# One core, 128 tiles of attention and a feed-forward layer with experts: q, k and up projections made for two tiles at a time

## What is computed

```
x = x + layernorm(attention(layernorm(x)))
x = x + layernorm(ffn(layernorm(x)))

attention(h):  q, k, v = h @ w_q.T, h @ w_k.T, h @ w_v.T
  sq, sk = elu(q) + 1, elu(k) + 1
  memory part: (sq @ memory) / (sq @ memory_norm)
  local part, chunk by chunk of 128 rows: A = (sq @ sk.T) * causal mask
     (A @ v + sq @ S) / (sum(A) + sq @ z);  then S += sk.T @ v, z += sum(sk)
  output (gate mix of the two) @ w_o.T
ffn(h):  silu(h @ W_up.T) @ W_down.T                       (256 -> 1024 -> 256)
       + product-key experts: 4 heads, top 8 of 1024 each,
         weights silu((h . down_embed) * softmax(scores)), sum of up_embed rows
```

## Time and profile before

| | |
|---|---|
| median of 3 runs | 2856.78 us (2856.33 to 2860.16) |
| profiled run: its time, its span | 2860.13 us, 2858.4 us |
| PE, PEld busy | 99%, 80% of the span |
| ACT, DVE, POOL busy | 88%, 85%, 72% of the span |
| granted TensorE clock | 0.998 of full |
| DMA, bytes moved | 471.58 MB, mean 165 GB/s |

### The profile page before, as it was taken

One profiled execution on the slowest core, in us unless ns is written; L12 is line 12 of the kernel. 1 busy time (PEld: TensorE's weight loads), 2 busy tenths in 40 slices (PEclk: granted clock), 3 DMA queues, 4 the chain that ended last, 5 costly groups with the idle time before them and its releaser, 6 DMA issues.

```text
span 2858.4 us, 48065 instructions
## 1 busy us (share of the span) xinstructions
PE 2829.4 (99%) x14724; PEld 2294.9 (80%) x14724; DVE 2424.2 (85%) x6125; ACT 2525.0 (88%) x3618; POOL 2055.1 (72%) x2460
## 2 busy tenths in 40 slices
PE   8899999999999999999999999999999999999999
PEld 6688788878888888888788878888888788788877
DVE  5888888888888888888888888888888888888886
ACT  5888998899888989888998898888989888998997
POOL 3677777777777777777777777777777777777674
PEclk9999999999999999999999999999999999999999
DMA  4576667766766766676667766666767676667664
GB/s 120 140 174 166 166 172 172 167 169 169 170 165 170 171 168 167 169 173 167 165 172 173 167 168 170 168 166 170 171 168 167 169 173 166 167 171 171 151 152 120
DMA packets 450053, 471.58 MB, mean 165 GB/s; under 512 B 234883, under 2 KB 384516, under 8 KB 449796
## 3 DMA queue, kind: packets, MB, share of 16 engines
q0 software_dynamic: 52832, 199.77, 36.1%
q1 hardware_dynamic: 396964, 268.74, 31.1%
HBM read 137.37 MB, written 131.20 MB: 94 GB/s over the span
## 4 chain that ended last, share of the span: by engine, by line
PE 95%; ACT 1%; DVE 1%; issue 1%; POOL 1%; DMA 1%; SPq 0%; POOLq 0%; DVEq 0%; ACTq 0%
PE banks L684 89%; PE banks L828 4%; PE banks L810 2%; POOL sums L532 0%; DMA g_parts<-w_way 0%; DVE w_blocks L1117 0%; DVE prob L1109 0%; DMA wexp<-wexp 0%; ACT prob L979 0%; PE banks L619 0%; PE banks L627 0%; PE banks L641 0%; DMA w_way<-w_blocks 0%; PE banks L661 0%; PE banks L698 0%
## 5 line engine op out<-in xcount | busy, mean ns | idle before, releaser
L532 POOL TENSOR_TENSOR sums<-scores 128x1024 f32<-128x1024 f32 x512 | 1002.3, 2037 | 76.0 <-ACT scores L1018 76.0
L518 POOL TENSOR_TENSOR rstd<-var_eps,minus_half 128x1 f32<-128x1 f32 x512 | 501.9, 980 | 43.0 <-ACT y_sq L928 15.3
L684 PEld LDWEIGHTS banks<-xn2T,wupT 128*128 128x128 f32 x4096 | 484.0, 188 | 9.4 <-DVE state L1171 3.0
L684 PE MATMUL banks<-xn2T,wupT 128*128 128x128 f32 x4096 | 486.2, 274 | 2.1 <-DVE state L1171 2.1
L684 PE MATMUL banks<-deT,xn2T 128*128 128x512 f32 x1024 | 484.4, 596 | 2.4 <-DVE picked L1064 2.0
L684 PE MATMUL banks<-ue,gT 128*128 128x256 f32 x2048 | 462.8, 379 | 0.3 <-ACT gT L957 0.3
L684 PE MATMUL banks<-wdownT,hT 128*128 128x256 f32 x2048 | 462.8, 379 | 0.2 <-ACT y_sb L1014 0.2
L684 PEld LDWEIGHTS banks<-wdownT,hT 128*128 128x128 f32 x2048 | 389.0, 190 | 56.8 <-issue 3.0
L684 PEld LDWEIGHTS banks<-ue,gT 128*128 128x128 f32 x2048 | 388.7, 190 | 52.7 <-ACT gT L957 0.7
L570 POOL TENSOR_TENSOR wexp<-wexp,w_last 128x1 f32<-128x1 f32 x127 | 131.6, 1036 | 385.1 <-ACT z_last L1007 385.1
L684 PEld LDWEIGHTS banks<-deT,xn2T 128*128 128x128 f32 x1024 | 191.9, 197 | 130.9 <-issue 121.2
(11 more groups left out here) (162 smaller groups left out, 6661.2 us busy)
## 6 DMA issues: line engine op xcount, KB each, us to landing
wexp<-wexp POOLq DMA_DIRECT2D x127, 1024.0 KB, 9.1
wexp<-wexp POOLq DMA_DIRECT2D x127, 512.0 KB, 4.7
w_way<-w_blocks SPq DMA_DIRECT2D x127, 512.0 KB, 2.6
g_parts<-w_way SPq DMA_DIRECT2D x508, 128.0 KB, 4.9
xn_way<-xn_blocks SPq DMA_DIRECT2D x248, 128.0 KB, 1.8
x_in<-_attn_hidden_states_dram SPq DMA_DIRECT2D x128, 128.0 KB, 2.2
out_dram<-x_out SPq DMA_DIRECT2D x128, 128.0 KB, 1.8
xn1T<-xn_way SPq DMA_DIRECT2D x500, 32.0 KB, 2.2
```

Source lines behind the costliest of these rows:

```text
L518: return nc.gpsimd.tensor_tensor(rstd[:, n, m:m + 1], var_eps[:, n, m:m + 1], minus_half[:, :], ALU.pow)
L532: return nc.gpsimd.tensor_tensor(sums[:, k, :, :], scores[:, k, 0:XIN].unsqueeze(2).broadcast_to([P, XIN, NKEYS]), scores[:, HEADS + k, :] ...
L684: last = nc.tensor.matmul(out, lhs(c), rhs(c), start=(start and c == 0), stop=(stop and c == chunks - 1))
```

## The change

Three things are done. `PAIRED = 6`: from tile 6 on, tiles (t, t+1) with t even share their q, k and up products, so that an instruction moves 256 columns, the two tiles lying side by side in `xn1T` and `xn2T` (now 4 buffers each, `TURNED`). An even turn of stage 7 makes k for tiles t and t+1; an odd one makes q for t+1 and t+2. The even and the odd turn of stage 10 each make one half of the up product for both tiles of the pair, up to tile 125. Second, `ahead(t, stage)` gives the chain of the first norm the tile of stage-1 instead of stage: from tile 5 on, `xn1` is normed, turned and gathered one turn earlier. Third, on SyncE the gather of `xn2T` stands before `sk_way` and `g_parts`.

```diff
+        def q_buffer(t):
+            return 1 if t < PAIRED else 1 + ((t - PAIRED) // 2 + 1) % 2
+        def ahead(t, stage):
+            old, new = t[stage], t[stage - 1]
+            if old is not None and old < AHEAD:
+                return old
+            return new if new is not None and new > AHEAD else None
+        def paired_up(t):
+            return PAIRED <= t < LATE
...
# SyncE
+            def xn1_in(x):
+                moved(sp, s_xn1_blocks_out, x, 1, TILES, EARLY)
+                wait(sp, s_v_in_psum, x + 1 - TURNED)
+                gather(xn1T[:, x % TURNED, :, :]..., xn1_way[x % 2, :, :], s_xn1_blocks_in[x % 2])
...
# TensorE
+            def up(t, half):
+                if not paired_up(t):
+                    for k in range(4):
+                        ic = 4 * half + k
+                        last = product(u_ps[half][:, k * P:(k + 1) * P], DC, lambda c: wupT[:, c, ic * P:(ic + 1) * P],
+                                       lambda c: xn2T[:, t % TURNED, :, c])
+                else:
+                    first = t // 2 * 2 % TURNED
+                    for k in range(2):
+                        ic = 4 * (t % 2) + 2 * half + k
+                        last = product(two_tiles(u_ps[half])[:, k, :, :], DC, lambda c: wupT[:, c, ic * P:(ic + 1) * P],
+                                       lambda c: xn2T[:, first:first + 2, :, c])
+                return last
+            def two_tile_q_or_k(dst, w, t):
+                for ec in range(DC):
+                    last = product(two_tiles(dst)[:, ec, :, :], DC, lambda c: w[:, c, ec * P:(ec + 1) * P],
+                                   lambda c: xn1T[:, t % TURNED:t % TURNED + 2, :, c])
+                return last
...
+                    if paired_up(u) and u % 2 == 0:
+                        moved(pe, s_xn2_blocks_in, u + 1, BLOCKS, LATE, EARLY)
...
-                    early(pe, 'xn1', t[7])
-                    moved(pe, s_xn1_blocks_in, t[7], BLOCKS, TILES, EARLY)
+                    if t[7] < PAIRED:
+                        early(pe, 'xn1', t[7])
+                        moved(pe, s_xn1_blocks_in, t[7], BLOCKS, TILES, EARLY)
+                    elif t[7] % 2 == 1:
+                        moved(pe, s_xn1_blocks_in, t[7] + 1, BLOCKS, TILES, EARLY)
+                        moved(pe, s_xn1_blocks_in, t[7] + 2, BLOCKS, TILES, EARLY)
...
+                    elif t[7] % 2 == 0:
+                        two_tile_q_or_k(qk_ps, wkT, t[7]).then_inc(s_qk_in_psum, 1)
+                    elif t[7] < TILES - 1:
+                        two_tile_q_or_k(qk_ps, wqT, t[7] + 1).then_inc(s_qk_in_psum, 1)
```

More of the change, by code:

```diff
@@ L437, in body @@
                         sp.dma_start(xn2_way[t[8] % 2, :, :], xn2_blocks[:, :]).then_inc(s_xn2_blocks_out[t[8] % 2], 16)
[L438 to L441, removed]
+                x = ahead(t, 5)
+                if x is not None:
+                    if x >= EARLY:
+                        xn1_out(x)
                 if t[11] is not None:
@@ L445, in body @@
                         sp.dma_start(w_way[t[11] % 2, :, :], w_blocks[:, :]).then_inc(s_expert_weights_blocks_out[t[11] % 2], 16)
+                if t[8] is not None:
+                    if EARLY <= t[8] < LATE:
+                        moved(sp, s_xn2_blocks_out, t[8], 1, LATE, EARLY)
+                        wait(sp, s_up_0_in_psum, t[8] - 2)
+                        gather(xn2T[:, t[8] % TURNED, :, :].rearrange('p (i t) c -> p i (t c)', t=BLOCK), xn2_way[t[8] % 2, :, :], s_xn2_blocks_in[t[8] % 2])
                 if t[7] is not None:
@@ L454, in body @@
                         gather(g_parts[:, :, :, :].rearrange("p i c t -> p i (c t)"), w_way[t[11] % 2, :, :], s_expert_weights_blocks_in[t[11] % 2])
[L455 to L464, removed]
+                if x is not None:
+                    if x == AHEAD + 1:
+                        xn1_in(AHEAD)
+                    if x >= EARLY:
+                        xn1_in(x)
                 if t[0] is not None:
@@ L711, in body @@
                         turn_wdown(0, 0)
-                    if t[10] == TILES - 3:
+                    if u == TILES - 3:
                         turn_xn('xn2', xn2, s_xn2_ready, LATE)
-                    if t[10] == TILES - 2:
+                    if u == TILES - 2:
                         turn_xn('xn2', xn2, s_xn2_ready, LATE + 1)
[L716 to L728, removed]
+                    if paired_up(u) and u % 2 == 0:
+                        moved(pe, s_xn2_blocks_in, u + 1, BLOCKS, LATE, EARLY)
@@ L739, in body @@
                         turn_xn('xn2', xn2, s_xn2_ready, 2)
-                    early(pe, 'xn1', t[7])
-                    moved(pe, s_xn1_blocks_in, t[7], BLOCKS, TILES, EARLY)
-                    wait(pe, s_hidden_1_ready, t[7] - 2)
+                    if t[7] == PAIRED:
+                        pe.wait_ge(s_set_sb, SET_ALL)
+                        moved(pe, s_xn1_blocks_in, PAIRED, BLOCKS, TILES, EARLY)
+                        moved(pe, s_xn1_blocks_in, PAIRED + 1, BLOCKS, TILES, EARLY)
+                        two_tile_q_or_k(first_q_ps, wqT, PAIRED).then_inc(s_first_q_ps, 1)
+                    if t[7] < PAIRED:
[4 more added lines that the diff above has]
+                        moved(pe, s_xn1_blocks_in, t[7] + 2, BLOCKS, TILES, EARLY)
+                    wait(pe, s_hidden_1_ready, up_done(t[7] + 7), TILES)
                     if not steady:
                         wait(pe, s_state_ready, t[7] - 1, KEPT)
[L745 to L749, removed]
+                    if t[7] < PAIRED:
+                        for n, w in enumerate((wkT, wqT)):
+                            for ec in range(DC):
+                                col = (n * DC + ec) * P
+                                last = product(qk_ps[:, col:col + P], DC, lambda c: w[:, c, ec * P:(ec + 1) * P],
+                                               lambda c: xn1T[:, t[7] % TURNED, :, c])
+                        last.then_inc(s_qk_in_psum, 1)
+                    elif t[7] % 2 == 0:
+                        two_tile_q_or_k(qk_ps, wkT, t[7]).then_inc(s_qk_in_psum, 1)
+                    elif t[7] < TILES - 1:
+                        two_tile_q_or_k(qk_ps, wqT, t[7] + 1).then_inc(s_qk_in_psum, 1)
                     if t[7] == 0:
```

249 lines of the change are left out of this document (170 added, 79 removed).

## The result

| | before | after |
|---|---|---|
| median | 2856.59 us (2856.33 to 2860.16, 4 runs) | 2979.72 us (2972.73 to 2984.65, 4 runs) |
| ratio, 95% interval | | 1.0426 [1.0401, 1.0451] |
| profiled run: its time, its span | 2860.13, 2858.4 us | 2976.63, 2974.9 us |
| granted TensorE clock | 0.998 | 0.994 |

A forecast was written before the change was run, and what follows sets the result against it. The prediction took TensorE to bound the kernel: 2860.1 us profiled, less 31 saved by wide instructions, plus 84 of waits at q, gives 2913 us, or 2910 against the median; range 2855 to 2950 us.

The forecast's parts named there:

- What bounds the kernel: TensorE, busy 1999.93 of 2000 us mid-run: shortening its stream shortens the run, any wait lengthens it in full.
- What the wide instructions save: In TensorE's up, q and k products, one 256-column record replaces two of 128, saving 11 ns each, 31 us together.
- the full 11 ns: Saving per pair of up, q or k records, from the expert sum's 216 ns against 227 for two of 128.
- Its lower end: Bottom of the range for the saving in up, q and k: no gain at all.
- The reordered `xn2T`: On SyncE, moving xn2T's gather forward makes up's new wait cost nothing, with some 4 us to spare.
- The wait at q: In 60 odd turns TensorE's q waits 1.40 us for xn1T's gather, landing 4.86 us behind the head: 84 us.
- the rival of the longer-held queue: Moved xn2T issues fill SyncE's queue, g_parts leaves 0.5 to 0.7 us later, wait 2.1 us: 2952 us, chance 0.15.
- the loop can't absorb the wait: k's end to gather's landing takes 21.3 us, TensorE's way to q 19.9, so the wait recurs every odd turn.
- The sum: Whole kernel: 2860.1 us less 31 saved plus 84 waited gives 2913 us, or 2910 against the median.
- The rival of the small saving: Up, q and k save only 5 ns a pair, 14 us, with the q wait present: 2927 us, chance 0.12.
- the range: Forecast time of the whole kernel, 2855 to 2950 us, leaving out the fast case and the held queue's far end.

The follow-up runs named there:

- e7: The kernel before, without pairing, with xn1T and xn2T stored as [half, row] so that moving columns are adjacent: 2850.49 us, ratio 0.997.
- e5: e1 with the paired q, k and up products reading 256 adjacent numbers, so partly wrong results: 2836.41 us, ratio 0.9916.
- e3: The changed kernel with the gather of xn2T put back behind g_parts, ahead of xn1T: 3293.0 us in a single run.
- e1: The changed kernel with SyncE's gather of xn1T right behind that of xn2T, ahead of sk_way and g_parts: 2863.99 us, ratio 1.0013.
- e2: The changed kernel with GpSimd's first accumulating transfer (1 MB) at half its columns, leaving out part of the result: 2861.13 us in a single run.
- e6: e1 with xn1T and xn2T stored as [half, row], columns adjacent and right, each norm's blocks written out in 4 transfers, not 1: 3053.75 us, ratio 1.0675.
- e4: The changed kernel with the v product ahead of the paired q in odd turns: 2976.5 us, ratio 1.0408.
- e10: e1 with only xn2T stored as [half, row] and the store of x_out behind the two gathers, a step later: 2841.43 us, ratio 0.9934.

## Why the prediction was wrong

**What bounds the kernel** held: what TensorE saved or waited in the middle turns showed in the time.

**What the wide instructions save: 31 us predicted, 2 to 3 measured.** This step failed, at the sentence "I take the full 11 ns, since the expert sum is the nearest row in size and whatever the step costs is already in up's 113 ns". The expert sum's columns are adjacent. The measured table (start to start, ns) is 111.6 and 215.8 for 128 and 256 adjacent columns, 113.4 and 226.7 at a step of two [e7, e5; before, after]. So of the step only 1.8 ns were in the 113, and 10.9 are in the 227 of a wide record: it takes back all that the width gives. The 11 ns that the prediction took for the width are 7.4 for the width (2 x 111.6 - 215.8) and 3.6 for the step, and both need adjacent columns. The prediction took the row nearest in width where it needed the one nearest in layout. Its lower end, no gain at all, was all but right.

**The reordered `xn2T`: free** held. It lands 17.3 us behind the head of the turn before, with 4.5 us to spare, and e3 shows what the old place costs.

**The wait at q: the mechanism held, the size did not.** Landing 4.86 us behind the head was forecast from `xn2T`'s old place; the median is 5.1, with a tail up to 6.7. The wait is 103 us over the run, 1.7 us an odd turn, for 84 and 1.40. Part is what I had given the rival of the longer-held queue: `g_parts` lands at 4.06 us, 3.60 before. e1 and e2 show the cause, the megabyte, from both sides. That the loop can't absorb the wait held.

**What was missing: the slower records behind a wait, about 16 us,** most of them at half clock. The sum priced a wait at its own length.

So against the profiled runs: 103 + 16 - 3 = 116 us, and 2976.6 - 2860.1 = 116.5 measured. Of the 63 us between forecast and that, 28 are the saving, 19 the wait and 16 the slower records: three errors of one sign. The rival of the small saving kept 14 us of it, and none joined the bounds of two terms; the range ended at 2950 for that reason.

## What to carry to other kernels

Before an edit that makes matmuls wider, compare the spacing of records with the same step between moving columns, not just the same width: here wider instructions at a step of two gained 2 to 3 us, and the same with adjacent columns 23. When a product starts to need its data earlier, look for the first large transfer of any queue that is issued ahead of the gather's last issue: here `xn2T`'s last issue stood 0.5 us ahead of it in the kernel of 2841 us and 1.2 us behind it in that of 3054. And price a wait on a saturated TensorE above its length: it cost 1.2 times that in the change, whose waits were 1.8 us long on average, and 1.5 to 1.6 times in e6 and e3, with 2.5 and 4.8 us.

## What the runs showed of the hardware

- A float32 record whose moving columns stand two numbers apart takes 1.6% longer than one of adjacent columns at 128 columns (113.4 against 111.6 ns), and 5% at 256 (226.7 against 215.8). One record of 256 in place of two of 128 saves 7.4 ns when the columns are adjacent and 0.1 at a step of two.
- A wait of 2.44 us ended in 3.4 us of granted clock 0.50; of the 53 waits of 3.9 to 6.6 us in e3's 106 turns 45 came with 6.8 us of it and 8 with 3.4. In e4, where q waited 1.05 us an odd turn, two such stretches occurred in the 106 turns, at waits of 2.15 and 2.17 us.
- The 32 KB parts of a gather that are issued in the 3.5 us ahead of the megabyte, or up to 0.8 us behind its issue, land 1.6 to 2.6 us later (in e10, from 200 to 2400 us, 414 of 414 and 197 of 199). Those issued 1.2 us or more behind it, while it is under way, mostly land with it (at most 0.3 us earlier) or after it: 97 of 101 in e10, 358 of 384 after the change, 346 of 458 in e6. So the later they are issued, the shorter they seem to take: 6.8 us at 1.2 us behind (e6), 3.2 us at 7.4 us behind (the gather ahead of the q product at 1526.09).
